# Moving y's second half by one token with DMA transfers instead of two matmuls, in front of a feed-forward norm

## What is computed

```
h = shift_token(y);  q, k, v = split(h @ wqkv)
q, k = rotary(l2norm(q) * qs, l2norm(k) * ks)
y = y + local_attention(q, k, v) @ wo            # 8 heads, windows of 128 tokens
h = shift_token(y)                               # the place of the change
h = (h - mean) / sqrt(var + 1e-5) * lg + lb
a, g = split(h @ w1 + b1)
y = y + (a * gelu(g)) @ w2 + b2
```

## Time and profile before

| what | value |
|---|---|
| time, median of 3 runs | 1166.75 us (1166.71 to 1169.32) |
| span of the profiled execution | 1166.5 us |
| PE busy | 1131.5 us, 97% of the span |
| DVE busy | 832.4 us, 71% |
| ACT busy | 709.4 us, 61% |
| POOL busy | 612.1 us, 52% |
| the chain that ended last | PE 88%, DVE 5%, ACT 4%, issue 1%, POOL 1% |
| DMA, hardware queue of SP | 40448 packets, 80.20 MB, 22.1% of 16 engines |

### The profile page before, as it was taken

One profiled execution on the slowest core, in us unless ns is written; L12 is line 12 of the kernel. 1 busy time (PEld: TensorE's weight loads), 2 busy tenths in 40 slices (PEclk: granted clock), 3 DMA queues, 4 the chain that ended last, 5 costly groups with the idle time before them and its releaser, 6 DMA issues.

```text
span 1166.5 us, 20317 instructions
## 1 busy us (share of the span) xinstructions
PE 1131.5 (97%) x6858; PEld 895.1 (77%) x6858; DVE 832.4 (71%) x2481; ACT 709.4 (61%) x1744; POOL 612.1 (52%) x641
## 2 busy tenths in 40 slices
PE   8899999999999999999989999999999999999997
PEld 6777877887788776577757887877878878777676
DVE  6788777878787556668887767768666777674553
ACT  3678777778776513543576756556666466575832
POOL 1455657565654311129786646538456465573330
...
GB/s 270 40 53 139 167 129 164 153 167 129 163 113 69 181 19 55 1 95 36 19 159 16 1 1 1 127 1 2 1 19 97 55 1 1 1 14 60 20 37 19
DMA packets 40549, 81.48 MB, mean 70 GB/s; under 512 B 5888, under 2 KB 18304, under 8 KB 39936
## 3 DMA queue, kind: packets, MB, share of 16 engines
q1 hardware_dynamic: 40448, 80.20, 22.1%
...
## 4 chain that ended last, share of the span: by engine, by line
PE 88%; DVE 5%; ACT 4%; issue 1%; POOL 1%; DMA 0%; SPq 0%; DVEq 0%; ACTq 0%; POOLq 0%
PE psum L1551 53%; PE psum L1649 6%; PE psum L1631 5%; PE psum L1781 5%; PE psum L1830 5%; PE psum L1815 4%; PE psum L1797 4%; PE psum L1763 2%; ACT probs L909 1%; DVE probs L1156 1%; PE psum L1558 1%; PE psum L1737 1%; PE psum L1843 1%; PE psum L1854 1%; POOL probs L751 1%
## 5 line engine op out<-in xcount | busy, mean ns | idle before, releaser
L751 POOL TENSOR_TENSOR probs<-probs,rden 128x128 f32<-128x128 f32 (+3 forms) x256 | 178.1, 728 | 79.1 <-DVE rden L1168 79.1
L909 ACT ACTIVATE probs<-probs,negmax 128x128 f32<-128x128 f32 (+3 forms) x256 | 140.7, 552 | 14.2 <-DVE negmax L1163 13.6
L993 ACT ACTIVATE lp<-lp,lneg,rn 128x256 f32<-128x256 f32 (+1 forms) x256 | 143.6, 568 | 9.0 <-DVE lneg L1385 8.9
L1156 DVE CUSTOM_DVE_ANT_0 probs<-psum,causal 128x512 f32<-128x512 f32 (+3 forms) x256 | 109.9, 485 | 15.3 <-PE psum L1551 14.8
L784 POOL TENSOR_TENSOR lp<-lp,lrden 128x128 f32<-128x128 f32 x64 | 25.7, 401 | 166.4 <-DVE lrden L1390 166.4
L796 POOL TENSOR_TENSOR rn<-ssm,neg_half 128x8 f32<-128x8 f32 x64 | 108.5, 1696 | 0.0
L1373 DVE CUSTOM_DVE_ANT_0 lp<-psum,local 128x256 f32<-128x256 f32 (+1 forms) x256 | 84.1, 385 | 19.5 <-PE psum L1781 19.5
L787 POOL TENSOR_TENSOR lp<-lp,lrden 128x768 f32<-128x768 f32 x64 | 94.0, 1468 | 0.0
L874 ACT ACTIVATE pT<-psum 128x512 f32<-128x512 f32 (+1 forms) x96 | 47.1, 518 | 66.5 <-PE psum L1631 66.2
L1631 PE MATMUL psum<-ident,probs 128*128 128x128 f32 x640 | 85.4, 273 | 1.2 <-POOL probs L751 1.2
L1551 PE MATMUL psum<-q,k_rest 128*128 128x256 f32 (+2 forms) x256 | 85.3, 344 | 1.1 <-DMA k<-k_round 0.6
...
## 6 DMA issues: line engine op xcount, KB each, us to landing
k<-k_round SPq DMA_DIRECT2D x128, 128.0 KB, 2.4
...
```

The costliest lines, as they stand in the source:

```text
L751: ins = pool.tensor_tensor(pr, pr, rden[:, u % 2, h, i:i + 1].broadcast_to([P, TRI[i]]), ALU.mult)
L909: ins = act.activation(pr, pr, ACT.Exp, bias=negmax[:, u % 2, h, i:i + 1], scale=ADH ** -0.5, accum_out=den[:, u % 2, h, i:i + 1])
L993: ins = act.activation(pr, pr, ACT.Exp, bias=lneg[:, u % 2, h, w:w + 1], scale=rn[:, m % 2, w, 0, 2 * j + h:2 * j + h + 1], accum_out=lden ...
L1156: ins = dve.tensor_tensor_reduce(probs[:, u % 2, h, TRI_AT[i]:TRI_AT[i + 1]], bank[:, at:at + TRI[i]], causal[:, S - TRI[i]:S], 1.0, -3e38 ...
```

## The change

The `sh` pieces leave PE's order, and so do the matrix `shift` and its load. SP gets a function `move_half(m)` of three transfers from y to the second half of the tile `hn`: rows 0 to 126 to rows 1 to 127 for all four tiles (127 partitions, 4 runs of 128 floats each), row 127 of tiles 0 to 2 to row 0 of tiles 1 to 3, and one row of zeros from DRAM. DVE waits for all three (`y_moved`), takes bn_stats of hn's second half where it lies, and normalises it in place. The PSUM bank of `sh` is no longer taken, so the turns of group `g` fall otherwise. The written orders are new; around the change, PE now has Sa of the next step directly behind `wo` and before v, and Sa3 before k2.

```
-    shift = np.zeros((P, 2, P), np.float32)
-    shift[:, 0, :] = i == j - 1
-    shift[P - 1, 1, 0] = 1.0
+    ... "c_zero": np.zeros((1, P), np.float32)
...
+            def move_half(m):
+                b = m % B
+                for tp in range(2):
+                    wait_read(sp, plan["wo", m, tp])
+                sp.dma_start(hn[1:P, :, P:D], y[0:P - 1, b, :, P:D]).then_inc(y_moved, 16)
+                sp.dma_start(hn[0:1, 1:T, P:D], y[P - 1:P, b, 0:T - 1, P:D]).then_inc(y_moved, 16)
+                sp.dma_start(hn[0:1, 0, P:D], a["c_zero"]).then_inc(y_moved, 16)
...
             def mlp_norm(m):
-                bank = wait_full(dve, plan["sh", m])
+                dve.wait_ge(y_moved, 3 * 16 * (m + 1))
                 for t in range(T):
-                    dve.bn_stats(stats[:, 0, t, 6:12], bank[:, t * P:(t + 1) * P]).then_inc(f_stats, 1)
+                    dve.bn_stats(stats[:, 0, t, 6:12], hn[:, t, P:D]).then_inc(f_stats, 1)
...
             def mlp_apply(m):
-                    ins = dve.tensor_scalar(hn[:, t, P:D], bank[:, t * P:(t + 1) * P], mv[:, 0, t, 0:1],
-                                            rstd[:, 0, t:t + 1], ALU.subtract, ALU.mult)
-                ins.then_inc(read[use[0]], 1)
+                    dve.tensor_scalar(hn[:, t, P:D], hn[:, t, P:D], mv[:, 0, t, 0:1], rstd[:, 0, t:t + 1],
+                                      ALU.subtract, ALU.mult)
...
-            def shifted_half(m):
-                mm(bank ..., shift[:, 0, :], y[:, m % B, :, P:D], ...)
-                mm(bank ..., shift[:, 1, :], y[:, m % B, 0:T - 1, P:D], ...)
...
-        STEP_PE = (... wo0 wo1 v0@2 sh Tb0@1 v1@2 Sa2@1 AV0@1 Sb2@1 Tqk0@2")
+        STEP_PE = (... wo0 wo1 Sa2@1 v0@2 Tb0@1 v1@2 AV0@1 Sb2@1 Tqk0@2")
-        CLOSE_DVE = (... T.28.0 wo.6.0 wo.6.1 stats.6 norm.6 T.28.1 Sa.30 apply.6 ...
+        CLOSE_DVE = (... wo.6.0 wo.6.1 T.28.0 stats.6 T.28.1 norm.6 Sa.30 apply.6 ...
```

More of the change, by code:

```diff
@@ L274, in build @@
         set1 = sem("set1")
-        ld_shift = sem("ld_shift")
+        y_moved = sem("y_moved")
         hid_one, last_gate = sem("hid_one"), sem("last_gate")
@@ L310, in unit_at @@
             return c, j, j // 2, 2 * c + j % 2
-        START_PE = ("xT.0 pv.0 pk.0 pq.0 xT.1 pv.1 xT.2 s.0.0 s.0.1 pk.1 pq.1 pv.2 t.0.0 pv.3 s.1.0 "
[4 rows of a table removed]
-        START_DVE = ("xs.0 xn.0 xT.0 aw.0.0 xs.1 aw.0.1 aw.0.2 xs.2 xn.1 xn.2 pk.0 pq.0 xT.1 s.0.0 xs.3 "
[4 rows of a table removed]
[L324 to L330, removed]
+        START_PE = ("xT.0 pv.0 pk.0 pq.0 xT.1 pv.1 xT.2 s.0.0 s.0.1 pk.1 pq.1 pv.2 t.0.0 pv.3 s.1.0 t.0.1 "
[3 rows of a table added]
+        START_DVE = ("xs.0 xn.0 xT.0 aw.0.0 xs.1 aw.0.1 aw.0.2 xs.2 xn.1 xn.2 pk.0 pq.0 xT.1 s.0.0 xs.3 s.0.1 "
[4 rows of a table added]
+        START_ACT = ("xT.0 aw.0.0 aw.0.1 aw.0.2 pv.0 pk.0 pq.0 xT.1 xT.2 pv.1 e.0.0 pk.1 pq.1 e.0.1 pv.2 pv.3 "
+                     "t.0.1 e.1.0 t.0.3 pk.2 t.0.5 e.1.1 pq.2 t.1.1 t.1.3 t.1.5 pk.3 e.2.0 pq.3 e.2.1 pv.4 "
+                     "t.2.1 e.3.0 pk.4 pq.4 t.2.3 t.2.5 e.3.1 t.3.1 e.4.0 t.3.3 pk.5 t.3.5 xT.3 pq.5 e.4.1 "
+                     "pv.5")
+        START_POOL = ("ln.0 ln.1 ln.2 ln.3 f.0.0 f.0.1 f.1.0 f.1.1 f.2.0 f.2.1 f.3.0 f.3.1 f.4.0 f.4.1 f.5.0 "
+                      "part.0 f.5.1 f.6.0 part.1 f.6.1 part.2 f.7.0 f.7.1 f.8.0 part.3 f.8.1 f.9.0 part.4 "
+                      "f.9.1 part.5")
         UNIT_PE = ("t0 s0@1 t1 t2 s1@1 pk@2 t3 t4 t5 pq@2 z pv@2")
@@ L385, in build @@
[L385 to L388 removed]
[6 rows of a table removed]
[L395 to L398 removed]
+        ENTRY_PE = ("s.29.0 t.28.0 t.28.1 s.29.1 t.28.2 pk.30 pq.30 t.28.3 t.28.4 t.28.5 pv.30 z.28 s.30.0 "
[9 rows of a table added]
@@ new lines, in build @@
+        ENTRY_DVE = ("s.29.0 s.29.1 t.28.0 t.28.2 r.29.0 pk.30 t.28.4 pq.30 r.29.1 z.28 s.30.0 s.30.1 t.29.2 "
[8 rows of a table added]
+        ENTRY_ACT = ("t.28.1 e.29.0 pk.30 pq.30 t.28.3 t.28.5 e.29.1 pv.30 e.30.0 pk.31 t.29.1 t.29.3 t.29.5 "
[8 rows of a table added]
+        ENTRY_POOL = ("f.29.0 f.29.1 f.30.0 f.30.1 f.31.0 f.31.1 norm2.0 norm2.1 kvs.0 norm2.2 kvs.1 y.0 "
[4 rows of a table added]
+        STEP_PE = ("q2@1 hnT@-1 v2@1 Sa3 k2@1 Ta1 hid0@-1 Tb1 hid1@-1 Tqk1@1 Sb3 hid2@-1 q3@1 hid3@-1 k3@1 "
+                   "Tqk2@1 hid4@-1 hid5@-1 AV1 Ta2 v3@1 hT@2 w20@-1 Tqk3@1 q0@2 Tb2 Sa0@1 AV2 Sb0@1 k0@2 "
+                   "Ta3 q1@2 w21@-1 Tb3 k1@2 Sa1@1 AV3 Sb1@1 Ta0@1 wo0 wo1 Sa2@1 v0@2 Tb0@1 v1@2 AV0@1 "
+                   "Sb2@1 Tqk0@2")
@@ new lines, in build @@
+        STEP_DVE = ("Tqk3 Tb2@-1 Sa0 fb3@-1 q0@1 w20@-2 Sb0 k0@1 Ta3@-1 q1@1 w21@-2 Tb3@-1 fa0 Sa1 k1@1 Sb1 "
[3 rows of a table added]
+        STEP_ACT = ("Tqk0@1 AV0 q2@1 v1@1 hnT@-1 ea2 k2@1 Ta1 v2@1 eb2 Tb1 hid0@-1 hs0@-1 hid1@-1 Tqk1@1 "
+                    "hid2@-1 hs1@-1 hs2@-1 q3@1 hid3@-1 k3@1 Tqk2@1 hs3@-1 hid4@-1 hid5@-1 hs4@-1 hs5@-1 Ta2 "
+                    "ea3 hT@2 eb3 Tqk3@1 AV1 q0@2 Tb2 v3@1 k0@2 q1@2 Ta3 AV2 ea0@1 Tb3 k1@2 AV3 eb0@1 Ta0@1 "
+                    "ea1@1 Tb0@1 v0@2 eb1@1")
+        STEP_POOL = ("k3@1 fb2 fa3 fb3 q0@2 fa0@1 k0@2 fb0@1 fa1@1 norm fb1@1 q1@2 k1@2 q2@2 k2@2 fa2@1 q3@2")
@@ new lines, in build @@
+        CLOSE_PE = ("T.29.0 hnT.6 T.29.1 Sa.31 w1.6.0 w1.6.1 Sb.31 AV.29 T.30.0 w1.6.2 T.30.1 w1.6.3 w1.6.4 "
+                    "AV.30 T.31.0 wo_early.7.0 T.31.1 w1.6.5 AV.31 wo_early.7.1 wo.7.0 wo.7.1 w2.6.0 hnT.7 "
+                    "w2.6.1 w1.7.0 w1.7.1 w1.7.2 w1.7.3 w1.7.4 w1.7.5 w2.7.0 w2.7.1")
+        CLOSE_DVE = ("Tqk.7.3 soft.27.1 T.26.1 w2.5.0 Sa.28 T.27.0 Sb.28 T.27.1 soft.28.0 Sa.29 w2.5.1 Sb.29 "
[6 rows of a table added]
+        CLOSE_ACT = ("T.29.0 AV.28 hnT.6 T.29.1 exp.30.0 w1.6.0 w1.6.1 exp.30.1 T.30.0 exp.31.0 AV.29 hs.6.0 "
+                     "w1.6.2 w1.6.3 T.30.1 exp.31.1 AV.30 T.31.0 w1.6.4 hs.6.1 T.31.1 w1.6.5 hs.6.2 hs.6.3 "
+                     "AV.31 hs.6.4 hs.6.5 hnT.7 w1.7.0 hs.7.0 w1.7.1 w1.7.2 w1.7.3 hs.7.1 w1.7.4 hs.7.2 "
+                     "hs.7.3 w1.7.5 hs.7.4 hs.7.5")
@@ L399, in build @@
         CLOSE_POOL = ("sum.0 soft.30.1 soft.31.0 soft.31.1 last.6 norm.7 last.7 sum.1")
-        MLP = ("stats", "sh", "norm", "apply", "hnT", "hT")
+        MLP = ("stats", "norm", "apply", "hnT", "hT")
         def step_items(cycle, m):
@@ L519, in build @@
                     plan["w1a", at[0], at[1]] = plan["w1g", at[0], at[1]]
-            if what == "sh":
-                turn(("sh", *at), "g")
             if what == "Tqk":
@@ L706, in _ @@
             layer_wqkv_hi(1, 2)
-            for tp in range(2):
-                wait_read(sp, plan["wo", B - 1, tp])
+            move_half(2)
+            move_half(3)
             layer_wo(1)
@@ L714, in _ @@
             layer_w2(1)
+            move_half(4)
+            move_half(5)
             wait_full(sp, plan["v", STEPS - 1, T - 1])
@@ L718, in _ @@
                 sp.dma_start(x2[:, b, :, :], x2_dram[b].rearrange("(t p) e -> p t e", p=P)).then_inc(x2_ld[b], 16)
+            move_half(6)
+            move_half(7)
             for b in range(B):
@@ L1423, in mlp_apply @@
                 dve.wait_ge(f_rstd, m + 1)
-                use = plan["sh", m]
-                bank = psum[use[0]]
                 for t in range(T):
-                    ins = dve.tensor_scalar(hn[:, t, P:D], bank[:, t * P:(t + 1) * P], mv[:, 0, t, 0:1],
-                                            rstd[:, 0, t:t + 1], ALU.subtract, ALU.mult)
-                ins.then_inc(read[use[0]], 1)
+                    dve.tensor_scalar(hn[:, t, P:D], hn[:, t, P:D], mv[:, 0, t, 0:1], rstd[:, 0, t:t + 1],
+                                      ALU.subtract, ALU.mult)
                 for t in range(T):
@@ L1833, in output_part @@
                     ins.then_inc(full[use[0]], 1)
-            def shifted_half(m):
-                if m == 0:
-                    pe.wait_ge(ld_shift, 16)
-                for tp in range(2):
-                    wait_read(pe, plan["wo", m, tp])
-                use = plan["sh", m]
-                bank = wait_free(pe, use)
-                mm(bank[:, :].rearrange("p (t e) -> p t e", e=P), shift[:, 0, :], y[:, m % B, :, P:D], start=True,
-                   stop=False, skip_group_check=True)
-                mm(bank[:, P:T * P].rearrange("p (t e) -> p t e", e=P), shift[:, 1, :], y[:, m % B, 0:T - 1, P:D],
-                   start=False, stop=True, skip_group_check=True).then_inc(full[use[0]], 1)
             def transposed_norm(m):
@@ L1929, in _ @@
                     output_part(*at, range(FPAIRS - 1, FPAIRS) if at[0] == STEPS - 1 else range(FPAIRS))
-                if what == "sh":
-                    shifted_half(*at)
                 if what == "hnT":
```

27 lines of the change are left out of this document (3 added, 24 removed), and 94 rows, old and new, of tables (CLOSE_DVE, ENTRY_ACT, ENTRY_DVE, ENTRY_PE).

## The result

| | before | after |
|---|---|---|
| median of 4 runs, us | 1168.03 (1166.71 to 1171.31) | 1282.05 (1280.25 to 1284.23) |
| ratio, 95% interval | | 1.0968 (1.0941 to 1.0994) |
| span of the profiled execution, us | 1166.5 | 1279.5 |
| granted clock in the page's 40 slices | 9 (90% or more) in each | 7 or 8 in 9 of them |
| end of y's addition to bn_stats of the moved half, step 2 | 2.20 | 14.95 |

The change makes the kernel 9.7% slower. The page's parts of the changed kernel: the granted clock in 40 slices, the chain by engine, and two groups of instructions (busy, mean ns, then the idle time before them and what ended it).

A forecast was written before the change was run, and what follows sets the result against it. PE was taken to bound steps 1 to 5, with DVE's wait for the move holding it up. From 1166.75 us, 105.4 of net waits and 13.6 of clock gave 1286 us, range 1240 to 1345.

The forecast's parts named there:

- What bounds the kernel: Steps 1 to 5: PE, busy 76.00 of 76.00 us; sh's 1.51 us saved, any PE wait added in full.
- One engine: The move's first transfer, 127 partitions: all 508 pieces on one DMA engine, 14.7 us; chance 0.83.
- The price of a piece: Each 512 byte piece of the move's first transfer: 29 ns, bounds 24 and 48 ns.
- The fixed part: Move's time besides the 508 pieces: 0.05 us to issue, 1.35 to land, 0.1 for queueing.
- The third transfer: Last of the move's three transfers: issued 0.37 us after the second.
- The wait moved to AV and Tqk: PE waits at AV in steps 1 to 5, 12.93 us more each; at Tqk in step 0, +12.9.
- The clock: Behind each of eight PE stalls the granted clock falls: 1.7 us each, 13.6 us in all.
- Orders at nothing: Edits besides the move, whole kernel: no time gained or lost.
- The rival of 16 engines: All 16 engines share the first transfer: move ready 3.1 us after y, total 1167.5 us, not slower; chance 0.11.
- the point of no loss: A move ready 3.3 us after y breaks even; below it the change gains, some 6 us at 2.3.

The follow-up runs named there:

- e3: Kernel before, with its sh matmuls and without the move, given the changed kernel's order lists: 1170.53 us, ratio 1.0015 to the kernel before.
- e1: Changed kernel with the move's first transfer cut into one of 112 partitions and one of 15: 1184.88 us, ratio 1.0133 to the kernel before.
- e2: Changed kernel with the move's first transfer cut into one of 124 partitions and one of 3: 1219.49 us, ratio 1.0431 to the kernel before.
- e5: Changed kernel with its three transfers issued in opposite order, the large one last: 1285.09 us, ratio 1.0999 to the kernel before.
- e10: e1 plus 8 unread identity matmuls on PE ahead of the first AV of steps 2 to 6: 1177.56 us, ratio 1.0098 to the kernel before.
- e6: e1 with DVE's waiting bn_stats placed behind the second lpT copy and the maxima of Sa: 1168.26 us, ratio 1.0001 to the kernel before.

## Why the prediction was right

Predicted 1286 us, measured 1282.05. By its own steps:

- **What bounds the kernel** held: PE's wait in a step was added in full. Step 2: 75.93 before, + 0.26 orders (e3), - 1.51 `sh`, + 12.94 wait, + 1.55 for AV at half clock (3.22 for 1.67) = 89.17 us, and the trace has 89.24. The copy to lpT, which the prediction put at 0.54 us by the earlier trace rows, has 0.50 there; it changes nothing.
- **One engine** was the step on which all hung, and it held: share 6.7% of 16 after, against nearly all engines at 112 partitions and two tenths at 124. The Trainium skill (DMA: Bandwidth & Descriptors, section "Why a DMA increments its semaphore by 16 and not by 1") states that a transfer uses as many engines as the largest number up to 16 that divides the slowest dimension of both sides; the runs agree for 127, 124 and 112.
- **The price of a piece** was put at 29 ns: busy 28.0, but one each 25.4 ns, 13.0 us for 14.7. The fixed part was put at 1.5 us and is 1.95: 0.08 to the issue, some 1.2 to the first packet, 0.65 from the last packet to DVE. Ready 14.95 for 16.2 us, 1.25 us less; steps 1 to 5 came in 0.88 us less each (13.75 for 14.63), since the clock and the orders took part of it back. The 142 ns for 2 KB, a quarter of which was 35.5, was the wrong neighbour for one lone engine, but the right one for a shared transfer (32 and 33 ns in e1 and e2).
- **The third transfer** was put at 0.37 us behind the second. It was issued 11.4 us after the first. That was a wrong picture which cost 0.4 us at most (e5).
- **The wait moved to AV and Tqk**, as said: 17.52 us from `wo` to AV for the predicted 18.82. In step 7 it stands at the transposes of hn, as said too; in step 6 at the scores ahead of them, which wait for DVE's maxima:

```profile
1173.73 2.08 PE L1781 MATMUL psum<-lkT,lqT 64*128 64x256 f32 x8 [13.95 <-DVE lmax L1376]
```

- **The clock** was put at 1.7 us per stall and was undersized. The earlier trace rows themselves give 1.5, since PE was busy for only 1.02 us of the first window. Measured, the work lost is 1.5 to 2.8 us in each of steps 1 to 5 (mean 1.97) and 22.6 us from y.0 to the end, against 1.7 in the kernel before: 20.8 us more, where 13.6 was forecast, though in the close not all of it need lie on the chain.
- **The total is nearer than its terms.** The waits were 8 x 1.25 = 10 us too long in the forecast, the clock some 7 us too small. That they nearly cancel, and 1286 meets 1282.05, is luck; the mechanism is not.
- **Orders at nothing** was nearly right in a step, +0.26 us, and wrong in the close: y.6 to y.7 is 17.3 us longer where 15.4 was forecast and the shorter ready time should have given 14. The clock falls twice in this stretch (5.5 us of work lost). The new lists of the close are worth 4.1 us in e3's profiled execution and some 0.4 over its runs, so how much of the 17.3 is theirs stays open.
- **The rival of 16 engines** was mis-sized, though it did not come. It set ready at 3.1 and the point of no loss at 3.3 us. Such a split is ready at 3.92 us (e1) and loses 15.6 us, for the most part because it left out the clock: e1 loses 14.9 us of PE's work to it behind y.0, the kernel before 1.7. With `sh` gone PE stands at AV 3.86 us after y and AV starts 1.86 us after the statistics, so any ready time over 2.0 us makes PE wait; a wait of 1.9 us was paid with 1.65 us more for the clock in three of e1's five steps, one of 0.12 us (e10) in none. What took the loss away was not a faster move but DVE's order (e6).

Not settled: the 0.3 us per step that e6 is above the sum; why e5's later issue shows by 0.67 of 1.06 us only; why the clock falls behind a wait of 1.9 us in three steps and not in two; and what the move alone costs in the close.
